# Routing joined to the attention block of a mixture-of-experts layer: earlier first queries and keys, tables made in the first slots, a tournament for the group sums

## What is computed

```
xn = layernorm(x)
# attention: 16 heads of 32, one shared key/value head, rotary positions with a decay, causal
q, kv = xn @ w_q.T, xn @ w_kv.T ;  out = softmax(rot(q) rot(k)^T + mask) v @ w_proj.T + b_proj
# experts: 32 experts in 4 groups of 8; per token the best 2 groups, in them the best 8 experts
scores = sigmoid(xn @ gate_w.T) ;  sb = scores + gate_bias
group_scores = sum of the top 2 of each group of sb ;  keep the 2 best groups
topi = top 8 of what is kept ;  wsel = scores[topi] / sum * 2.5
routed = sum_e cw_e * (relu2((xn @ fc1.T) @ w1_e) @ w2_e) @ fc2.T
shared = relu2(xn @ up.T) @ down.T
y = x + attention + shared + routed
```

## Time and profile before

| | us |
|---|---|
| median of 3 runs (lowest to highest) | 1913.45 (1913.42 to 1913.49) |
| the profiled execution, device time | 1912.29 |
| its span in the trace | 1910.7 |
| PE busy / DVE busy / ACT busy / POOL busy | 1708.0 / 1197.3 / 900.2 / 840.3 |

### The profile page before, as it was taken

The page is one execution under the profiler, slowest core; times in us unless marked ns, Lnnn a source line. Parts: engine busy times, 40 slices in busy tenths (PEclk is TensorE's granted clock), DMA queues, the critical chain, the costliest instruction groups (busy, mean ns, idle before and its releaser), DMA issues. The chain is left out here.

```text
span 1910.7 us, 37850 instructions
## 1 busy us (share of the span) xinstructions
PE 1708.0 (89%) x10116; PEld 1374.0 (72%) x10116; DVE 1197.3 (63%) x3631; ACT 900.2 (47%) x2470; POOL 840.3 (44%) x719
## 2 busy tenths in 40 slices
PE   5801889999999899899998999899999999999979
PEld 5801776776767767767677676588888888888866
DVE  7776675766767767667576675355555555555547
ACT  2320664764656647656566476233333333333322
POOL 0053242332433423333334343377777776777740
PEclk9955999999999999999999999899999999999989
DMA  7983333433333324333333331688888888887749
GB/s 287 361 292 46 91 121 94 129 108 111 123 103 110 122 94 127 113 125 110 114 101 112 105 122 62 166 152 159 148 164 151 150 157 176 178 172 130 124 141 365
DMA packets 188531, 277.91 MB, mean 145 GB/s; under 512 B 34120, under 2 KB 130639, under 8 KB 185140
## 3 DMA queue, kind: packets, MB, share of 16 engines
q0 software_dynamic: 60528, 92.74, 24.1%
q1 hardware_dynamic: 72724, 117.19, 20.4%
q10 hardware_dynamic: 55088, 65.67, 11.2%
HBM read 124.08 MB, written 132.04 MB: 134 GB/s over the span
## 5 line engine op out<-in xcount | busy, mean ns | idle before, releaser
L1404 POOL DMA_INDIRECT sums<-e_y,e_where x288 | 448.0, 1556 | 215.0 <-DMA sums<-e_y,e_where 89.9
L756 POOL DMA_INDIRECT slot_rows<-m_row,m_idx x256 | 268.1, 1047 | 567.4 <-ACT m_sc L808 474.8
L808 ACT ACTIVATE m_sc<-m_sc,m_low 128x512 f32<-128x512 f32 (+3 forms) x512 | 283.8, 556 | 170.1 <-DVE m_low L938 140.8
L938 DVE CUSTOM_DVE_ANT_0 m_sc<-m_psS,cst 128x512 f32<-128x512 f32 (+3 forms) x512 | 230.3, 486 | 145.4 <-PE m_psS L1092 142.6
L1434 PE MATMUL e_psH<-e_w,e_xt 128*128 x1152 | 297.9, 381 | 0.6 <-SPq L1256 0.6
L1434 PE MATMUL e_psY<-e_w,e_ht 128*128 x1152 | 296.3, 380 | 0.0
L1109 PE MATMUL m_psT<-cst,m_sc 128*128 128x128 f32 x1280 | 201.9, 279 | 32.2 <-ACT m_pt L819 28.2
L1305 ACT ACTIVATE e_xt<-e_psX 128x256 f32<-128x256 f32 x288 | 110.3, 383 | 224.3 <-PE e_psX L1423 184.4
L1434 PEld LDWEIGHTS e_psH<-e_w,e_xt 128*128 128x128 f32 x1152 | 197.4, 191 | 16.1 <-issue 1.0
L1434 PEld LDWEIGHTS e_psY<-e_w,e_ht 128*128 128x128 f32 x1152 | 196.4, 190 | 15.0 <-issue 0.2
L1310 ACT ACTIVATE e_ht<-e_psT 128x256 f32<-128x256 f32 x288 | 110.4, 383 | 204.7 <-PE e_psT L1448 182.9
(11 more groups left out here) (192 smaller groups left out, 3171.9 us busy)
## 6 DMA issues: line engine op xcount, KB each, us to landing
e_row<-slot_rows ACTq DMA_DIRECT2D x288, 144.5 KB
m_qs<-m_qhi SPq DMA_DIRECT2D x256, 64.0 KB, 2.0
e_w<-in_w SPq DMA_DIRECT2D x64, 256.0 KB
f_xt<-in_x SPq DMA_DIRECT2D x8, 1024.0 KB, 9.7
xnt_hi<-f_hi SPq DMA_DIRECT2D x8, 1024.0 KB, 4.3
xnt_lo<-f_lo SPq DMA_DIRECT2D x8, 1024.0 KB, 8.2
sums<-empty POOLq DMA_DIRECT2D x32, 256.0 KB, 2.5
m_qs<-m_qlo SPq DMA_DIRECT2D x128, 64.0 KB, 2.0
```

The lines of the kernel that those rows point to most:

```text
L756: pool.indirect_dma_start(out=xs, out_offset=bass.IndirectOffsetOnAxis(ap=idx[u][:, k:k + 1], axis=0), in_=row[u][:, :], in_offset=None).t ...
L808: nc.scalar.activation(cols, cols, ACT.Exp, bias=low[:, h % 2, i:i + 1], scale=-1.0, accum_out=total[:, h % 2, i:i + 1]).then_inc(exp_done, 1)
L938: nc.vector.tensor_tensor_reduce(out=sc[:, h % 2, SPC[i]:SPC[i] + n], in0=psS[k % 2][:, 0:n], in1=mask[:, S - n:S], scale=1.0, scalar=3.0e ...
L1404: pool.indirect_dma_start(out=both_sums, out_offset=bass.IndirectOffsetOnAxis(ap=where[u % NY][:, 0:1], axis=0), in_=y[u % NY][:, :], in_o ...
```

## The change

`routing` is no longer a block. Its steps become methods of a class `Routing`, and `middle` calls them at places in its own engines' orders. Their buffers lie in tiles of the middle that are unused at that time (the stages in `m_pt`, the scores in `m_ot`, and so on); pieces are 1024 columns instead of 2048, so there are 11 of them: wkv 1, wq 2, wup 4, wdown 4. Before `middle` only `front` is left, with its weight stage in `proj`.

What each engine does in the new block, in order: SP loads the bias, the pieces of wkv and wq, x of sequence 0, the pieces of wup and wdown (from the fifth on each waits for a low part three pieces back), then moves q0 (`stack(0, 0, -1)`), loads wproj and the bias of the projection, and stores the weights and the tables (waiting until they have landed) before `stack(0, 1)`. ACT makes the exponentials and seven high parts, copies q0 and kv, copies the totals from PSUM, makes the high halves of q0 and kv, and only then the high parts of wdown. PE makes q0, kv, the counts (`rank`), the turned values. DVE does `choose`, both rotations, both low halves, the values, `place`, then slot 0, after which `weigh` and `pads`, and after slot 1 `tables`. POOL makes the low parts, issues the first zeroing, then waits for slots, pads and the stored weights before its loop.

In `choose` the sum of a group's best two is a tournament on halves of 4, 2 and 1. In `place` the prefix over 32 tiles is three strided steps inside blocks of four tiles and then a chain over eight blocks; the prefix over experts has 16 zeros in front and so needs no copies. The triangle table is lowered by 1, so that the count of earlier tokens minus the tile's total comes out of PE and the inclusive prefix can be used.

```diff
-def routing(nc, xnt_hi, xnt_lo, xh, xlo, bias, cst, logits, rows, slots_sb, pads_sb, empty, xs, experts_dram, shifts_dram, halves, proj_in_sb, wproj):
...
+W = 1024
+R = 4
+class Routing:
+    def load_inputs(self, sp, halves):
+        sp.dma_start(self.bia, self.bias.partition_broadcast(P)).then_inc(self.b_in, 16)
+        for k, (dram, hi, lo, n) in enumerate(self.pieces):
+            if k == self.made["wq"]:
+                for to, src in halves:
+                    sp.dma_start(to[:, :, :].bitcast(F32), src[0]).then_inc(self.x_in, 16)
+            if k >= R:
+                sp.wait_ge(self.lo_made, k - R + 1)
+            sp.dma_start(self.stage[k % R][:, 0:n], dram).then_inc(self.landed[k % R], 16)
+    def save_tables(self, sp):
+        sp.wait_ge(self.named, 1)
+        sp.wait_ge(self.weighed, 1)
+        sp.dma_start(self.rows[:, LAT:ROW].rearrange("(g p) r -> p g r", p=P), self.tagged).then_inc(self.tagged_saved, 16)
+        sp.wait_ge(self.expert_made, 1)
...
+        sp.wait_ge(self.tagged_saved, 16)
+        sp.wait_ge(self.expert_saved, 64)
+    def high_parts(self, act, first, end):
+        for k in range(first, end):
+            dram, hi, lo, n = self.pieces[k]
+            act.wait_ge(self.landed[k % R], 16 * (k // R + 1))
+            self.nc.scalar.activation(hi, self.stage[k % R][:, 0:n], ACT.Copy).then_inc(self.hi_made, 1)
+    def rank(self, pe):
+        pe.wait_ge(self.picked_made, 1)
+        pe.wait_ge(self.rounded, 2)
+        for h in range(2):
+            half_g = slice(h * G // 2, (h + 1) * G // 2)
+            pe.matmul(self.totals[h], self.ones_r[:, :], self.picked_r[:, half_g, :], start=True, stop=True)
+            pe.matmul(self.ranks[h], self.tri_r[:, :], self.picked_r[:, half_g, :], start=True, stop=True).then_inc(self.counted, 1)
+    def choose(self, dve):
...
+        n = GE // 2
+        while n:
+            lower, upper = first[:, :, 0:n], first[:, :, n:2 * n]
+            if second is None:
+                nc.vector.tensor_tensor(to[0], lower, upper, ALU.max)
+                link(nc.vector.tensor_tensor(to[1], lower, upper, ALU.min))
+            else:
+                nc.vector.tensor_tensor(to[0], lower, upper, ALU.max)
+                nc.vector.tensor_tensor(between, lower, upper, ALU.min)
+                link(nc.vector.tensor_tensor(to[1], second[:, :, 0:n], second[:, :, n:2 * n], ALU.max))
+                link(nc.vector.tensor_tensor(to[1], between, to[1], ALU.max))
...
+            n //= 2
+        link(nc.vector.tensor_tensor(self.first_g, first.rearrange("p m e -> p (m e)"), second.rearrange("p m e -> p (m e)"), ALU.add))
...
+    def place(self, dve):
+        dve.wait_ge(self.totals_copied, 2)
+        block = inc.rearrange("p (b r) e -> p b r e", r=4)
+        for r in range(1, 4):
+            link(nc.vector.tensor_tensor(block[:, :, r, :], block[:, :, r, :], block[:, :, r - 1, :], ALU.add))
+        link(nc.vector.tensor_copy(offset[:, 1, :], block[:, 0, 3, :]))
+        for b in range(2, G // 4):
+            link(nc.vector.tensor_tensor(offset[:, b, :], offset[:, b - 1, :], block[:, b - 1, 3, :], ALU.add))
+        link(nc.vector.tensor_tensor(self.count, offset[:, G // 4 - 1, :], block[:, G // 4 - 1, 3, :], ALU.add))
...
+        for n, k in enumerate((1, 2, 4, 8, 16)):
+            a, z = self.tiles[n % 2], self.tiles[1 - n % 2]
+            link(nc.vector.tensor_tensor(z[:, 16:48], a[:, 16:48], a[:, 16 - k:48 - k], ALU.add))
...
+        nc.vector.tensor_copy(offset[:, 0, :], self.start)
+        link(nc.vector.tensor_tensor(offset[:, 1:G // 4, :], offset[:, 1:G // 4, :],
+                                     self.start.unsqueeze(1).broadcast_to([P, G // 4 - 1, E]), ALU.add))
+        link(nc.vector.tensor_tensor(block, block, offset.unsqueeze(2).broadcast_to([P, G // 4, 4, E]), ALU.add))
...
@@ middle, SP @@
+            routing.load_inputs(sp, ((xh, xnt_hi), (xlo, xnt_lo)))
+            stack(0, 0, -1)
+            sp.dma_start(wproj[:, :, :].rearrange("p c n -> p (c n)"), wproj_dram).then_inc(proj_in, 16)
             sp.dma_start(bp[:, :], bproj.partition_broadcast(P)).then_inc(bp_in, 16)
-            stack(0, 0, -1)
+            routing.save_tables(sp)
@@ middle, POOL @@
+            routing.low_parts(pool)
             for a in sums:
                 pool.dma_start(a[T:T + SPARE, :], empty[:, 0:LAT]).then_inc(zeroed, 16)
+            pool.wait_ge(routing.slots_made, 1)
+            pool.wait_ge(routing.pads_made, 1)
+            pool.wait_ge(routing.tagged_saved, 16)
+            pool.wait_ge(routing.tail_sent, 16)
@@ middle, ACT @@
+            n = routing.made["wup"]
+            routing.exponentials(act)
+            routing.high_parts(act, 0, n)
             for name in ("q0", "kv"):
                 copy_out(-1, name)
+            routing.copy_totals(act)
             for name in ("q0", "kv"):
                 high(-1, name)
+            routing.high_parts(act, n, len(routing.pieces))
...
+                    if s == 1 and first:
+                        act.wait_ge(routing.lo_made, len(routing.pieces))
@@ middle, DVE @@
+            routing.choose(dve)
             for name in ("q0", "kv"):
                 rotate(-1, name)
             for name in ("q0", "kv"):
                 low_part(-1, name)
             place_values(-1)
+            routing.place(dve)
...
+                    if first and s == 0:
+                        routing.weigh(dve)
+                        routing.pads(dve)
+                    if first and s == 1:
+                        routing.tables(dve)
@@ middle, PE @@
+            pe.wait_ge(routing.x_in, 32)
+            pe.wait_ge(routing.lo_made, routing.made["wq"])
             queries(-1, 0)
             project(-1, "kv", wkv_hi, wkv_lo)
+            routing.rank(pe)
             turn_values(-1)
@@ constant_table @@
-    c[:, COL["tri"]] = np.triu(np.ones((P, P)), 1)
+    c[:, COL["tri"]] = np.triu(np.ones((P, P)), 1) - 1
```

More of the change, by code:

```diff
@@ L91, in pipeline, with front @@
                 step(turns, s - lag)
-def front(nc, x, consts, fc1g, xnt_hi, xnt_lo, rows, cst, logits):
+def front(nc, x, consts, fc1g, xnt_hi, xnt_lo, rows, cst, logits, spare):
     with ExitStack() as ctx:
@@ L587, with middle @@
 U_AT = {n: k for k, n in enumerate(U_ORDER)}
-def middle(nc, x, bproj, xnt_hi, xnt_lo, xh, xlo, rows, wq, wkv, wproj, wup, wdown, cst, slots_sb, pads_sb, empty, xs, sums, partial):
+def middle(nc, x, bproj, xnt_hi, xnt_lo, xh, xlo, rows, wq, wkv, wproj, wup, wdown, cst, slots_sb, pads_sb, empty, xs, sums, partial,
+           logits, ot_flat, bias, experts_dram, shifts_dram, wproj_dram, weights):
     with ExitStack() as ctx:
@@ L621, in middle @@
         pt = sb("m_pt", [P, HC, NSP])
-        ot = sb("m_ot", [P, KC, S])
+        ot = ot_flat[:, :].rearrange("p (c s) -> p c s", c=KC)
         relu = sb("m_relu", [P, SHALF])
         sq = sb("m_sq", [P, SHALF])
-        sqhi = sb("m_sqhi", [P, 2, SHALF], F32R)
-        sqlo = sb("m_sqlo", [P, 2, SHALF], F32R)
+        sq_parts = sb("m_sq_parts", [P, 2, 2, SHALF], F32R)
+        sqhi, sqlo = sq_parts[:, 0, :, :], sq_parts[:, 1, :, :]
         res = sb("m_res", [P, TB, D])
@@ L659, in middle @@
         pidx_made = sem("m_pidx_made")
+        proj_in = sem("m_proj_in")
+        routing = Routing(nc, sb, sem, weights, bias, logits, rows, slots_sb, pads_sb, empty, xs, experts_dram, shifts_dram, cst,
+                          ot_flat[:, :], sc[:, :, :].rearrange("p a n -> p (a n)"), pt[:, :, :].rearrange("p a n -> p (a n)"),
+                          res[:, :, :].rearrange("p a n -> p (a n)"), rot[:, :], row[0][:, :],
+                          sq_parts[:, :, :, :].rearrange("p a b n -> p (a b n)").rearrange("p (g e) -> p g e", e=E),
+                          [t[:, :] for t in psT], [t[:, :] for t in psY])
         block = ctx.enter_context(nc.Block())
@@ L1065, in up @@
                     bank_free(b, f"up{s}")
+                    if first and s == 0:
+                        pe.wait_ge(routing.lo_made, routing.made["wup"])
                     for c in range(KC):
@@ L1071, in down @@
                 def down(s):
+                    if first and s == 0:
+                        pe.wait_ge(routing.lo_made, routing.made["wdown"])
                     pe.wait_ge(sqhi_made, at(b, NH, s + 1))
@@ L1158, in batch @@
                 pe.wait_ge(o_out, at(b, KC, KC))
+                if first:
+                    pe.wait_ge(proj_in, 16)
                 attention_result(b, 0)
```

421 lines of the change are left out of this document (186 added, 235 removed).

## The result

| | before | after |
|---|---|---|
| median, us (lowest to highest) | 1913.47 (1913.42 to 1915.66), 4 runs | 1899.92 (1894.83 to 1901.83), 4 runs |
| profiled execution / its span | 1912.29 / 1910.7 | 1900.54 / 1898.9 |
| first mask of the first sequence | 194.66 | 166.57 |
| first mask of the second sequence | 320.60 | 306.76 |

The ratio is 0.9922, 95% interval 0.991 to 0.9934: 13.5 us faster, where 26.0 were forecast; the time lies 3 us above the range. The first mask came at 166.57 for 166.5 forecast, 28.1 us earlier than before. Of these 28.1 us the first sequence gave back 14.3 and the rest of the program 2.0.

A forecast was written before the change was run, and what follows sets the result against it. One DVE chain was taken to bound the kernel up to the first mask. That mask 28.2 us earlier, less 2.2 added behind it, gave 26.0: 1912.29 - 26.0 = 1886.3 profiled, 1887.4 median, range 1878 to 1897.

The forecast's parts named there:

- Choosing and the tournament: DVE's choice of experts: tournament 4.84 us instead of 7.52, `picked` at 136.6, product with the scores 1.3 us, done at 137.9.
- Rotations and inputs: Both rotations on DVE, 2.8 us each, to 143.5, values placed at 145.2; q0 copied at about 131, kv at 137.
- the rival of the input chain: Before the keys' rotation: wup lands only with the tail at 139.2, rotation starts 6.3 us later; 1893.7 us, chance 0.13.
- Ranking, 13.3 us clean: DVE's ranking, from 145.2 to the slots: 13.3 us instead of 23.87, not counting the low parts beside it.
- Low parts beside it, 8.0: POOL's eight low parts of wdown beside the ranking's short DVE instructions: 1.06 us lost per meeting, 8.0 us taken.
- First mask 166.5: Start of head 0 in the first sequence: 145.2 + 13.3 + 8.0 = 166.5, which is 28.2 us earlier than 194.66.
- Added behind it, 2.2 of 6.7: DVE work moved into slots 0 and 1: weights and pads show 0.2 us, tables 2.0 of 2.6; bounds 0 and 6.7.
- SP's queue: Rival at head 4: weights' store takes 36.6 us, q1 moves late, 12 us more, 1899.4; some 8 us slack; chance 0.07.
- POOL's queue: Rival: first scatter at 193.8, 8.6 us later, some nine scatters behind; if POOL sets the middle's end, 1922.1; chance 0.03.
- The chance of 0.95 for faster: Sum for a faster kernel: forecast 0.62, low parts cheap 0.13, input chain 0.13, SP late 0.07.

The follow-up runs named there:

- the three edits with the first turn paced: Kernel after with weights right behind the choosing, low parts of wdown behind the last ranking step, first half turn of scatters spread: 1892.15 us, 0.984 of before.

## Why the prediction was wrong

1. *Choosing and the tournament*: right, and better. The tournament takes 4.3 us for 4.84; `picked` at 134.7, 1.9 us early. 1.1 of that is the instruction that makes it, 1.23 us for 2.35 before, since no low part was beside it. The product was mis-sized: 2.07 for 1.3, beside POOL's work.
2. *Rotations and inputs*: the queries were copied at 134.0, since wup's last piece landed at 133.07 instead of 129.0. This is the rival of the input chain at a tenth of its price: 0.7 us at the keys, inside what choosing had gained.
3. *Ranking, 13.3 us clean*: right. 13.7 in the run without low parts beside it (143.99 to 157.7), of which 0.44 is the slots' instruction with a low part beside it.
4. *Low parts beside it, 8.0*: 7.9 by that run. The Trainium skill ("SBUF — State Buffer", section "Who interferes with whom"), read as a low part's whole length for each (10.8), gives too much; the eight took 10.4 and cost 7.9. The placing does cost nearly what was forecast, and a wait puts it right.
5. *First mask 166.5*: 166.57. That it came so close is in part luck: the 1.9 us of step 1 were spent by the product, the late keys and small gaps. In seven more executions with the same chain it lay at 164.8 to 167.4.
6. *Added behind it, 2.2 of 6.7*: slots 0 to 2 gave back 3.7. The tables' eleven instructions show in full (2.7), since slot 1 has no idle time of DVE and what PE loses there it doesn't catch up. Mis-sized by 1.5 us.
7. *SP's queue*: mis-read. The 228.81 of the earlier trace rows is head 5's first mask; head 4's was 220.14, 25.5 us behind the first. So the slack was not 8 us but about 1, and q1 came 1.5 us late for PE. The landing of the weights (14.5 us) was right, but the tables' store landed 1.9 us behind it, and no term had it. The time of this rival was 1899.4, and 1899.92 was measured: that is chance, since its store of 36.6 us didn't come.
8. **The step that failed is POOL's queue.** It was looked at only as a rival for the end of the sequences, and there it was right: it catches up. How it catches up was costed at nothing, though the prediction itself had it nine scatters behind. Their due times are counted in exponentials, so a first scatter at 197.0, nearly four slots into the sequence (and 30.5 us behind the first mask, where it was 9.5 us ahead of it in the earlier trace rows), finds nine due at once. Two more fall due meanwhile and one for the pads stands between, so twelve run without a pause. On a chip with late increments that costs 9.2 us in slot 4 here, and 13.1 and 11.7 in two more executions of the same kernel; the first turn paced gives 6.7 us back (1896.38 to 1889.68), and the weights' store 20 us earlier 8.6 (to 1887.81).

At head 5 12.5 us are missing (26.0 - 13.5): 9.2 from step 8, 1.8 from step 7, 1.5 from step 6. The chance of 0.95 for faster held. On chip D the sum would have been right to 0.3 us for the medians, but this too is in part luck: in the two profiles there the second sequence starts 23.7 us earlier and the executions differ by 22.2. No row of before could tell that such chips exist; that scatters in a row go with waits of 3.55 us it could have told.

The best version on record is after with all scatters spread, weights behind the choosing, low parts behind the ranking and tables in slot 0: 0.9833 on chip D, 4.3 us ahead of after with spread scatters. On a chip with late increments it wasn't run; there the best are the scatters spread alone (0.9836, chip E) and the three edits with the first turn paced (0.984, chip C).

## What to carry to other kernels

A queue whose due times are counted in another engine's progress doesn't forget what is overdue: if its start is late, ask in what shape it catches up, and who is beside that burst. In this kernel the scatters into the slot list want a pause after every second one; those of the last block don't, so measure it. And a wait that ends on "remote" is a finding: look there for PE's increments, and see what GpSimd issues at that time, before blaming the waiting engine.

## What the runs showed of the hardware

- In the result's profiles and on four of the five chips PE's increments come late while GpSimd issues indirect scatters of 1156-byte rows back to back: with five, 87 of 93 times over 1.6 us, with twelve 12.06 to 13.14 us. In the last block, beside scatters that add 1024-byte rows, up to 15 in a row, none of 17185 does. On chip D none does at all, and the kernel before is 2.5% faster there (1866.45 for 1913.47). What differs between the chips isn't known, and neither is whether the tracing has a part: the traces with late increments lack a quarter of PE's increments beside those scatters, those of chip D under 1%.
- Spreading the scatters removes a part only. On chip E the kernel before so spread still has a second sequence of 125.6 us, for 120.1 on chip D.
- DVE loses about 1 us for each GpSimd instruction on two SBUF operands of 512 columns that meets it (7.9 for eight), though that instruction lasts 1.33.
